# Five items instead of three at the tail of a query convolution

## The reference, cut to what matters

```python
qkv = x @ w_qkv.T                               # q: 1024 channels, k: 256, v: 256
q = causal_conv1d(causal_conv1d(q, qc1_w, qc1_b, 16), qc2_w, qc2_b, 1)   # 3 taps; the second is dense, 1024 x 1024
k = causal_conv1d(causal_conv1d(k, kc1_w, kc1_b, 4), kc2_w, kc2_b, 1)
q = q.reshape(B, S, 16, 64) + 0.5 * k_mean[:, :, None, :]
k = k.reshape(B, S, 4, 64) + 0.5 * q_mean[:, :, None, :]
q, k = l2norm(q), l2norm(k) * key_temp
q, k = rope(q, cos, sin), rope(k, cos, sin)     # then attention
```

## Time and profile before

| | us |
|---|---|
| median of 3 runs | 2691.8 |
| the runs | 2689.99 to 2694.04 |
| the profiled execution | 2689.63 |
| its span, first to last instruction | 2687.8 |
| TensorE busy in the span | 2484.4 (92%) |
| the convolution block with its units (157 to 452 in the span) | 295 |

### The profile page before, as it was taken

How to read it: one execution, slowest core, us unless ns; L and a number is a source line. 1 busy time by engine, 2 the same in 40 slices (tenths; PEclk the granted TensorE clock), 3 DMA queues, 4 the chain that set the end, 5 groups by cost and what they waited for, 6 DMA issues and landing times. The chain is left out here.

```text
span 2687.8 us, 37367 instructions
## 1 busy us (share of the span) xinstructions
PE 2484.4 (92%) x12664; PEld 1813.3 (67%) x12664; DVE 1765.7 (66%) x3153; ACT 1420.0 (53%) x2796; POOL 1512.5 (56%) x1306
## 2 busy tenths in 40 slices
PE   7989995799799779999999999999999999999948
PEld 3464443444587667878878878878778878887734
DVE  2144454577423687777777777777777777777764
ACT  2200002656222286676676676676676676776603
POOL 0043365454101248678678678678678678678641
PEclk9999997899899899999999999999999999999978
DMA  4012320000210163353353342352352342352210
GB/s 162 0 38 75 117 63 32 1 1 1 86 51 21 64 194 105 89 158 100 94 158 97 97 157 95 100 154 93 102 156 91 100 158 91 99 161 91 69 47 32
DMA packets 143483, 241.86 MB, mean 90 GB/s; under 512 B 28352, under 2 KB 48576, under 8 KB 143168
## 3 DMA queue, kind: packets, MB, share of 16 engines
q1 hardware_dynamic: 143296, 239.48, 28.3%
HBM read 232.08 MB, written 7.34 MB: 89 GB/s over the span
## 5 line engine op out<-in xcount | busy, mean ns | idle before, releaser
L1755 ACT ACTIVATE mix<-mix,sc 128x128 f32<-128x128 f32 x1024 | 310.8, 389 | 3.0 <-DMA sc<-head_scal 3.0
L1925 DVE SCALAR_TENSOR_TENSOR feat<-ps,chan,feat 128x511 f32<-128x511 f32 (+2 forms) x384 | 283.7, 739 | 1.8
L2057 POOL TENSOR_TENSOR xend<-xdt,sc 128x384 f32<-128x384 f32 x128 | 107.0, 836 | 315.8 <-DVE xdt L1888 315.8
L98 PE MATMUL ps<-xt_hi,w_in_hi 128*128 128x512 f32 x640 | 266.9, 417 | 11.7 <-ACT sg L1745 3.5
L1914 DVE TENSOR_TENSOR mix<-mix,cb 128x512 f32<-128x512 f32 x256 | 270.6, 1062 | 1.2 <-ACT mix L1761 1.2
L99 PE MATMUL ps<-xt_lo,w_in_hi 128*128 128x512 f32 x640 | 253.2, 396 | 0.0
L100 PE MATMUL ps<-xt_hi,w_in_lo 128*128 128x512 f32 x640 | 253.1, 395 | 0.0
L2073 POOL TENSOR_TENSOR w_in_lo<-w_in_raw,w_in_hi 128x512 fp32r<-128x512 f32 x158 | 211.6, 1340 | 62.2 <-ACT w_in_hi L1710 62.2
L1959 DVE TENSOR_TENSOR y_lo<-y,y_hi 128x512 fp32r<-128x512 f32 x128 | 184.4, 1441 | 80.4 <-ACT y_hi L1771 80.1
L98 PE MATMUL ps<-xt_hi,w_g_hi 128*128 128x512 f32 x512 | 212.7, 415 | 4.6 <-DVE feat L1925 4.6
L1602 PE MATMUL ps<-w_o_hi,y_hi 128*128 128x512 f32 x512 | 206.9, 404 | 7.0 <-DVE x L1974 3.6
(11 more groups left out here) (278 smaller groups left out, 5946.3 us busy)
## 6 DMA issues: line engine op xcount, KB each, us to landing
mix<-row_cum SPq DMA_DIRECT2D x128, 512.0 KB, 5.7
w_in_raw<-in_w_conv_in SPq DMA_DIRECT2D x160, 256.0 KB, 3.0
w_g_raw<-in_w_gate_in SPq DMA_DIRECT2D x128, 256.0 KB, 3.4
ecb<-row_ecum SPq DMA_DIRECT2D x256, 96.0 KB, 3.4
w_o_raw<-in_w_out SPq DMA_DIRECT2D x64, 256.0 KB, 3.0
w<-in_w_c2q SPq DMA_DIRECT2D x16, 768.0 KB, 4.4
w<-in_w_c2q SPq DMA_DIRECT2D x16, 512.0 KB, 3.6
wqkv<-in_w_qkv SPq DMA_DIRECT2D x1, 3072.0 KB, 13.9
```

The source lines that it names most:

```text
L98: pe.matmul(out, a_hi, b_hi, start=(n == 0), stop=False)
L1755: last = act.activation(m, m, ACT.Relu, bias=sc[:, b, CUM, z, 2 * i + e:2 * i + e + 1], scale=-1.0)
L1925: dve.scalar_tensor_tensor(out=to, in0=ps[:, j % 2, 0:S - back], scalar=chan[:, bb % B, j, K1 - 1 - back:K1 - back], in1=to, op0=ALU.mult, ...
```

## The change

`TAIL` becomes 5 (`WS + EXTRA`): items 27 to 31 are taken group by group, items 0 to 26 whole. For five items to be at hand at once, the last two (30 and 31) get places of their own: their `tx` halves lie in `k1`, the taps of item 30 in `w2k` and those of item 31 in `head_sum[:, 0]`. Their preparation and their loads wait for `c2_ready` (all 8 groups of the key convolution) in place of `item_done`. SP issues its loads in the same order as before. The schedule, the units, the evictions and the number of matmuls stay.

```diff
-    NI = 4 * QT
+    NI, EXTRA = 4 * QT, 2
-            w2_loaded = [core.sem(f"a_w2_loaded{i}") for i in range(RAWS)]
+            w2_loaded = [core.sem(f"a_w2_loaded{i}") for i in range(RAWS + EXTRA)]
-            TAIL = WS
+            TAIL = WS + EXTRA
+
+            def last(r):
+                return r - (NI - EXTRA)
+
+            def tx_of(r, kind):
+                if last(r) < 0:
+                    return tx[:, r % WS, kind, :, :]
+                flat = k1[:, :, :, :].rearrange("p c b n -> p (c b n)")
+                at = (2 * last(r) + kind) * B * PAIRS
+                return flat[:, at:at + B * PAIRS].rearrange("p (b n) -> p b n", b=B)
+
+            def outer_taps(r):
+                if last(r) < 0:
+                    return w2[:, r % RAWS, 0:TAPS:2, :]
+                if last(r) == 0:
+                    return w2k[:, :, :, :].rearrange("p c t o -> p (c t o)")[:, 0:2 * BANK].rearrange("p (t o) -> p t o", t=2)
+                return head_sum[:, 0, :, :]
+
+            def loaded(eng, r):
+                if last(r) < 0:
+                    eng.wait_ge(w2_loaded[r % RAWS], 16 * (r // RAWS + 1))
+                else:
+                    eng.wait_ge(w2_loaded[RAWS + last(r)], 16)
+
+            def freed(eng, r):
+                if last(r) >= 0:
+                    eng.wait_ge(c2_ready, NK)
+                elif r >= WS:
+                    eng.wait_ge(item_done, r - WS + 1)
...
# SP, loads of the ring:
-                        if inner_item(r - RAWS):
+                        if last(r) >= 0:
+                            sp.wait_ge(c2_ready, NK)
+                        elif inner_item(r - RAWS):
...
-                            sp.dma_start(w2[:, r % RAWS, 0:TAPS:2, :], taps[:, 0:TAPS:2, :]).then_inc(w2_loaded[r % RAWS], 16)
+                            sp.dma_start(outer_taps(r), taps[:, 0:TAPS:2, :]).then_inc(
+                                w2_loaded[r % RAWS if last(r) < 0 else RAWS + last(r)], 16)
...
# TensorE, item(r, tiles):
                         if closing:
-                            pe.wait_ge(w2_loaded[r % RAWS], 16 * (r // RAWS + 1))
+                            loaded(pe, r)
...
-                                taps = w2[:, r % RAWS, 2 * kind, :] if closing else mixed[:, r % WS, kind, :]
-                                last = pe.matmul(ps[:, 2 * j + kind, :], tx[:, r % WS, kind, b, half * P:(half + 1) * P], taps,
+                                taps = outer_taps(r)[:, kind, :] if closing else mixed[:, r % WS, kind, :]
+                                done = pe.matmul(ps[:, 2 * j + kind, :], tx_of(r, kind)[:, b, half * P:(half + 1) * P], taps,
...
# VectorE and GpSimd, prepare(r):
-                        if r >= WS:
-                            dve.wait_ge(item_done, r - WS + 1)
+                        freed(dve, r)
...
-                        if r >= WS:
-                            pool.wait_ge(item_done, r - WS + 1)
+                        freed(pool, r)
```

More of the change, by code:

```diff
@@ L511, in item @@
                             for kind in range(2):
-                                taps = w2[:, r % RAWS, 2 * kind, :] if closing else mixed[:, r % WS, kind, :]
-                                last = pe.matmul(ps[:, 2 * j + kind, :], tx[:, r % WS, kind, b, half * P:(half + 1) * P], taps,
+                                taps = outer_taps(r)[:, kind, :] if closing else mixed[:, r % WS, kind, :]
+                                done = pe.matmul(ps[:, 2 * j + kind, :], tx_of(r, kind)[:, b, half * P:(half + 1) * P], taps,
                                                  start=(c == 0), stop=(c == QT - 1 and not closing))
                             if j == JT - 1:
-                                last.then_inc(item_done, 1)
+                                done.then_inc(item_done, 1)
                             elif c == QT - 1 and not closing:
-                                last.then_inc(pass_ready, 1)
+                                done.then_inc(pass_ready, 1)
                             if c == QT - 1 and closing:
@@ L521, in item @@
                                     tokens = head_sum[:, 1, b, half * 2 * P + e:(half + 1) * 2 * P:2]
-                                    last = pe.matmul(ps[:, 2 * j + e, :], tokens, sel[:, 0:BANK], start=False, stop=True)
-                                last.then_inc(pass_ready, 1)
+                                    done = pe.matmul(ps[:, 2 * j + e, :], tokens, sel[:, 0:BANK], start=False, stop=True)
+                                done.then_inc(pass_ready, 1)
                     for r in range(NI - TAIL):
@@ L535, in prepare @@
                         even, odd = q1[:, c, :, 0, :], q1[:, c, :, 1, :]
-                        if r >= WS:
-                            dve.wait_ge(item_done, r - WS + 1)
+                        freed(dve, r)
                         if inner_item(r):
-                            dve.tensor_tensor(tx[:, r % WS, 0, :, :], odd[:, :, 0:PAIRS], even[:, :, 1:], ALU.add).then_inc(t_one, 1)
+                            dve.tensor_tensor(tx_of(r, 0), odd[:, :, 0:PAIRS], even[:, :, 1:], ALU.add).then_inc(t_one, 1)
                             dve.wait_ge(ends_done, inner_before(r + 1))
@@ L544, in prepare @@
                         else:
-                            dve.tensor_tensor(tx[:, r % WS, 0, :, :], even[:, :, 0:PAIRS], even[:, :, 1:], ALU.subtract).then_inc(t_one, 1)
+                            dve.tensor_tensor(tx_of(r, 0), even[:, :, 0:PAIRS], even[:, :, 1:], ALU.subtract).then_inc(t_one, 1)
                     def evict(p, j):
@@ L664, in prepare @@
                             pool.tensor_tensor(ends[:, r % 2, :], w2[:, r % RAWS, 0, :], w2[:, r % RAWS, 2, :], ALU.add).then_inc(ends_done, 1)
-                        if r >= WS:
-                            pool.wait_ge(item_done, r - WS + 1)
+                        freed(pool, r)
                         if inner_item(r):
-                            pool.tensor_tensor(tx[:, r % WS, 1, :, :], even[:, :, 1:], odd[:, :, 0:PAIRS], ALU.subtract).then_inc(t_two, 1)
+                            pool.tensor_tensor(tx_of(r, 1), even[:, :, 1:], odd[:, :, 0:PAIRS], ALU.subtract).then_inc(t_two, 1)
                         else:
-                            pool.tensor_tensor(tx[:, r % WS, 1, :, :], odd[:, :, 1:], odd[:, :, 0:PAIRS], ALU.subtract).then_inc(t_two, 1)
+                            pool.tensor_tensor(tx_of(r, 1), odd[:, :, 1:], odd[:, :, 0:PAIRS], ALU.subtract).then_inc(t_two, 1)
                     def rope(u):
```

## The result

The changed kernel's first six executions have a median of 2681.9 us beside 2690.9 us for the kernel before; the ratio is 0.9967, with a 95% interval of 0.9955 to 0.9979. (One of the six, 2998 us at a granted clock of 0.79, was disturbed and is left out of the ratio; the median of the other five is 2680.5 us.) Two further measurements of the same kernel gave 0.9972 (0.9964 to 0.9981) and 0.9972 (0.9961 to 0.9983). Over the 24 undisturbed executions of the three measurements the median is 2683.0 us, against 2691.1 us for the 83 executions of before that were taken beside the experiments: **8.1 us or 0.30% faster**. The forecast was 7.6 us and 2684.2 us.

A forecast was written before the change was run, and what follows sets the result against it. Bound: in the query convolution's tail, group 0's readiness plus eight rotations on GpSimd. Item 31 starting at 395.45 instead of 403.06 gains 7.6 us; from the median of 2691.8 that gives 2684.2 us, range 2682.0 to 2688.8.

The forecast's parts named there:

- The bound and the chain: End of the query convolution: group 0's readiness plus eight rotations of 5.24 us sets the stage's end.
- Item 31 waits for GpSimd's queue: Tail, group 0: item 31 starts at 395.45 instead of 403.06, after its preparation behind unit 6; gain 7.6 us.
- The joint loads: SP's loads for items 29 to 31, issued together: the first lands after 4.3 us, worst case all after 6.8 us.
- The thin cover of group 1: Tail: group 1 takes 10.30 us against 10.48 us for two rotations; 0.32 us late, hidden by 0.62 us of slack.
- Rival (a): TensorE's clock falls in the 2.2 to 2.7 us gap before item 31; loss 1.6 us, 2685.8 us; chance 0.27.
- the third condition: Attention starts at the block's end, not at something fixed, so the whole 7.6 us gain moves with it.
- the range built on it: Whole kernel: 2682.0 to 2688.8 us, from the forecast's lower end over the low-clock case; before's three runs differ by 4 us.
- changed stages behind this one: Behind the query convolution: a changed stage length would show the prediction wrong; no size given.

The follow-up runs named there:

- experiment 5: Changed kernel with item 31's preparation put ahead of unit 6 on VectorE and GpSimd; ratio 0.9955 to the kernel before.
- experiment 6: Changed kernel with item 27's two matmuls done twice in each tail group; ratio 0.9988 to the kernel before.
- experiment 3: Changed kernel with EXTRA = 1, so four items (28 to 31) are taken group by group; ratio 0.9984 to the kernel before.
- experiment 7: Changed kernel with only the loads of items 30 and 31 issued earlier, ahead of that of item 26; ratio 0.9968 to the kernel before.
- experiment 1: Changed kernel again, no edit; median 2684.5 us beside 2691.3 us for the kernel before, ratio 0.9972.
- experiment 8: The kernel of experiment 4 again, no further edit; median 2678.7 us, ratio 0.9952 to the kernel before.
- experiment 4: Changed kernel with items 30 and 31 prepared right after item 26, loaded earlier, and 30 taken before 29; median 2680.2 us, ratio 0.9955 to before.
- experiment 11: Changed kernel a third time, no edit; median 2682.0 us beside 2690.7 us for the kernel before, ratio 0.9972.
- experiment 2: Kernel before measured against itself, no edit; ratio 0.9999.
- experiment 10: Kernel before with four additions into a dead buffer behind VectorE's last rotation; median 2689.8 us beside 2690.7 us, ratio 0.9998.

## Why the prediction came out as it did

**The bound and the chain were right.** The end of the stage is group 0's readiness plus eight rotations, as long as GpSimd is free by then (experiment 5) and the groups keep up (experiment 6). Relative to item 26 the terms came out as follows:

| after item 26 is done, us | forecast | measured |
|---|---|---|
| item 29, group 0 | 4.3 | 4.0 |
| item 30 | 6.0 | 5.8 |
| `tx` of item 31 ready | 9.9 | 9.97 |
| item 31 | 10.0 | 10.07 |
| eviction of group 0 | 13.7 | 13.78 |
| first tail rotation | 16.0 | 16.14 |
| attention's first transpose, before less after | 7.6 | 7.14 |

The agreement of 9.97 with 9.9 us for `tx` of item 31 is luck in part. I took unit 6 at 5.32 us on GpSimd and the preparation at 1.49 us; they took 5.72 us (395.71 - 389.99) and 1.03 us, two errors of 0.4 us with opposite signs.

**Item 31 waits for GpSimd's queue.** Experiments 3, 5 and 7 each move one thing: tail length, the order of preparations, the loads. In the first item 31 starts where GpSimd's queue puts it, in the second its gap is gone, and the third shifts nothing.

**The joint loads** were over-priced: the load for item 29 landed after 3.8 us, hardly later than a lone one, and those for items 30 and 31 after 4.8 and 5.8 us. Nothing hung on it.

**The thin cover of group 1 leaked.** I had 0.32 us of delay under 0.62 us of slack. Group 1 was evicted 10.30 us after group 0, as said, but its `ssc` step took 0.60 us instead of 0.23, so that its `rn` came 0.14 us late, and that `rn` took 1.85 us instead of 1.64:

```profile
413.63 1.85 POOL L708 TENSOR_TENSOR rn<-ssc,half 128x8 f32<-128x8 f32 x1
```

The last rotation began 37.08 us after the first (439.99 - 402.91) instead of 36.69. That is 0.4 us of the missing 0.5 us. It fits experiment 5, where the groups run further ahead and the last rotation begins 36.59 us after the first. That the longer steps are VectorE and GpSimd getting in each other's way was not tested.

**Rival (a) is real and is an outcome of single executions.** I gave it 0.27 and priced it at 1.6 us; it appeared in two of four profiles and cost 1.65 us. The Trainium skill, page "TensorE: Matmul & The Clock Gate", section "Why this matters for your kernels", warns of idle gaps between bursts of matmuls after which the clock is at half rate. These runs agree that it happens, and show it for shorter gaps than the page names: the clock fell after idling of 2.30, 2.35 and 2.65 us and stayed up after 2.44 and 2.46 us, so the length of the gap alone didn't decide. A case with chances is the right form for it; treating it as one kernel against another was not.

**The step that failed is the third condition, and the range built on it.** I let everything behind the stage move with its start and keep its length, a change of that length being taken at nothing, and took the scatter to be that of three executions of before. The prediction named changed stages behind this one as a sign of being wrong, and gave it no price. Measured, the attention block took 243.5 us in the first profile after and 250.9 us before, and its length differs from execution to execution with TensorE's granted clock. Same block, stretches of the first profile after and of experiment 1:

```profile
446.38:689.84 243.46, 204.63 (x961) 107.63 (x961) 153.88 (x505) 134.34 (x360) 109.36 (x151) 0.96 0.03 10
```

```profile
447.05:695.35 248.30, 210.24 (x960) 109.81 (x961) 153.94 (x505) 134.11 (x360) 109.11 (x151) 0.93 0.03 9
```

VectorE, ScalarE and GpSimd are busy alike to 0.25 us; TensorE is busy 5.6 us longer at 0.93 than at 0.96, and the block is 4.8 us longer. The difference can be placed. These are the stretches from 50 to 80 us behind the block's start, of the same two profiles in the same order:

```profile
496.38:526.38 30.00, 22.86 (x123) 11.90 (x124) 18.44 (x63) 19.91 (x53) 15.51 (x20) 1.00 0.00 1
```

```profile
497.05:527.05 30.00, 23.40 (x107) 11.88 (x107) 16.32 (x53) 17.05 (x45) 13.21 (x16) 0.83 0.00 1
```

In the four profiles with a block of 243.4 to 243.9 us the granted clock of this stretch is 1.00, in the nine others 0.77 to 0.83. The whole kernel's time goes with its mean clock: the changed kernel's executions at 0.974 have a median of 2679.6 us (5 of them), at 0.972 one of 2681.7 us (8), at 0.969 one of 2687.8 us (4). Before, 67 of 83 executions are at 0.969. So the changed kernel spreads over 13 us (2675.9 to 2689.0), before over 9, and a lower end 2.2 us under the forecast was far too near. (The prediction gives the end of the forecast's own range once as 2682.5 and once as 2682.0; the second is the one that its range uses.)

Of the 2.3 us between the forecast, 2684.2 us, and the first median, 2681.9 us, 0.9 us is the base: I subtracted from a median of 2691.8 us over three executions of before, and six gave 2690.9. The other 1.4 us is a gain of 9.0 instead of 7.6 us. That 8.1 us over all executions lies so near 7.6 is luck in part: the stage, which is all that I had summed, gave less, and what I had put at nothing gave the rest.

**What stays open.** 8.1 us were gained over all executions; the stage's rest gives 7.1 us or, with the clock's fall, 5.5 us. If the two halves of the profiles stand for all executions, that is 6.3 us, and some 2 us come from behind the stage. In four of the 13 profiles the attention block takes 243.4 to 243.9 us, all of them kernels that start it earlier than before (the first of after, experiments 5, 7 and 8). In the other nine it takes 247.1 to 251.3 us; the four with before's tail are among them, but so are executions with an early start (experiments 1, 4, 6 and 11). An earlier start is not by itself a shorter block: those that start at 440.79, 452.62 and 455.01 us (experiments 4, 2 and 10) took the same 249.6 to 249.8 us. What decides in an execution which length the block has stays open. Experiment 10 hints that shifting the start can be worth some 2 us; that the change's own shift is worth the remaining 2 us is argued, not shown.

## What to carry to other kernels

In a tail that feeds a slower follow-up chain, count from the time at which the first group is ready, and look for what that group's last operand waits for on every in-order queue; here it was the place of one preparation on GpSimd, and moving two preparations into an earlier idle stretch, with their loads ahead and item 30 taken before item 29, gave 3.5 us more than the change. A group may be made longer only up to the pace of the chain it feeds: 10.3 us under 10.5 us was free but for 0.4 us, 12.0 us cost 4.3 us. This kernel has stretches with idle gaps of 2 to 3 us on TensorE, and its time had several levels from execution to execution. Where you find such gaps, take the range of a forecast from the spread of many executions, and measure a few microseconds with ten or more on either side.

## What the hardware showed that I had not expected

The granted clock fell behind a gap of 2.30 us between full-pace matmuls in one execution and stayed at 1.00 across one of 2.46 us in another (of a kernel that differs in the order of its loads alone). Delaying the start of a block by 2.4 us left the kernel's time unchanged within what can be told (0.9998, 0.9989 to 1.0007); the quicker half of its executions had a higher mean clock, and no profile shows where. The attention block, the same work on the same operands, has one length when the granted clock is 1.00 from 50 to 80 us behind its start, 243.4 to 243.9 us, and takes 247.1 to 251.3 us when it is 0.77 to 0.83 there. Three 512 KB loads issued 0.4 to 0.5 us apart landed after 3.8, 4.8 and 5.8 us, the first as quickly as a load alone.
